# Score products ahead of the transposes of the weights, in every period of attention

## What is computed

```python
x = x + tanh(g_xattn[0]) * autocorrelation(layernorm(x), ctx, ctx)
x = x + tanh(g_ffn[0])   * routed_lora(layernorm(x))
x = x + tanh(g_xattn[1]) * attention(layernorm(x), ctx, ctx, mask)   # this one
x = x + tanh(g_ffn[1])   * fourier_ffn(layernorm(x))

# attention: 32 query heads, 8 key/value heads, width 128
q, k = rope(x @ wq), rope(ctx @ wk);  v = ctx @ wv
scores = einsum('bhgqd,bhkd->bhgqk', qg, k) / sqrt(128)
w = softmax(where(mask, scores, -1e9))
out = einsum('bhgqk,bhkd->bhgqd', w, v) @ wo
```

## Time and profile before

| | |
|---|---|
| median of 3 runs | 3050.01 us (3046.97 to 3050.73) |
| the profiled execution | 3049.93 us, of which the span is 3048.1 us |
| granted TensorE clock, mean | 0.994 of full speed |
| busy share: TensorE, VectorE, ScalarE, GpSimd | 98%, 65%, 41%, 42% |

### The profile page before, as it was taken

The page is one execution under the profiler, slowest core; times in us unless marked ns, Lnnn a source line. Parts: engine busy times, 40 slices in busy tenths (PEclk is TensorE's granted clock), DMA queues, the critical chain, the costliest instruction groups (busy, mean ns, idle before and its releaser), DMA issues.

```text
span 3048.1 us, 40952 instructions
## 1 busy us (share of the span) xinstructions
PE 2985.3 (98%) x14752; PEld 2502.7 (82%) x14752; DVE 1977.5 (65%) x4642; ACT 1256.4 (41%) x2626; POOL 1272.5 (42%) x1028
## 2 busy tenths in 40 slices
PE   9999999999999999999999999999999999999999
PEld 7888878887777878877888788888888888888887
DVE  4432478887665686678667877666766676666432
ACT  4111366665333422232224555554454445444220
POOL 2422388885322577768776333311111111111231
PEclk9999999999999999999999999999999999999999
DMA  7332421112555654455444776765566556575321
GB/s 247 127 122 97 170 57 63 70 56 100 175 193 194 194 167 111 111 157 159 111 111 125 226 239 227 242 215 169 181 206 202 181 174 218 175 272 174 136 91 56
DMA packets 317461, 479.91 MB, mean 157 GB/s; under 512 B 26108, under 2 KB 155516, under 8 KB 315468
## 3 DMA queue, kind: packets, MB, share of 16 engines
q1 hardware_dynamic: 316540, 475.84, 48.9%
q10 hardware_dynamic: 720, 1.44, 0.1%
HBM read 319.92 MB, written 157.29 MB: 157 GB/s over the span
## 4 chain that ended last, share of the span: by engine, by line
PE 56%; DVE 4%; DMA 2%; ACT 1%; POOL 1%; issue 0%; SPq 0%; ACTq 0%; DVEq 0%; POOLq 0%
PE PB L150 18%; PE PB L151 18%; PE PB L152 18%; PE PB L2383 3%; DMA at_wol<-wod 1%; DMA qp_raw<-in_wq 0%; PE PB L2682 0%; DVE qp_r L2179 0%; DMA qp_in<-xod 0%; DVE at_ptl L2522 0%; DVE at_ss L2502 0%; ACT at_ss L2430 0%; POOL qp_a L2209 0%; DVE qp_b L2142 0%; DVE qp_r L2187 0%
## 5 line engine op out<-in xcount | busy, mean ns | idle before, releaser
L2545 POOL TENSOR_TENSOR at_ql<-at_qf,at_qh 128x512 fp32r<-128x512 f32 x128 | 166.4, 1300 | 911.2 <-ACT at_qh L2423 911.2
L2430 ACT ACTIVATE at_ss<-at_ss,at_sm,at_bs 128x256 f32<-128x256 f32 x512 | 303.6, 594 | 334.8 <-DVE at_sm L2506 334.8
L150 PE MATMUL PB<-at_woh,at_ah 128*128 128x512 f32 x1024 | 400.8, 391 | 2.7 <-DMA at_wol<-wod 1.5
L151 PE MATMUL PB<-at_wol,at_ah 128*128 128x512 f32 x1024 | 399.9, 391 | 0.0
L152 PE MATMUL PB<-at_woh,at_al 128*128 128x512 f32 x1024 | 399.1, 390 | 0.0
L150 PE MATMUL PB<-qp_b,qp_a 128*128 128x512 f32 x896 | 350.0, 391 | 8.1 <-POOL qp_a L2209 2.6
L2536 DVE SCALAR_TENSOR_TENSOR at_xt<-PB,gt,at_xt 128x512 f32<-128x512 f32 x256 | 192.0, 750 | 251.7 <-PE PB L152 251.7
L152 PE MATMUL PB<-qp_b,qp_a 128*128 128x512 f32 x896 | 348.7, 389 | 0.0
L151 PE MATMUL PB<-qp_b,qp_a 128*128 128x512 f32 x896 | 348.7, 389 | 0.0
L2209 POOL TENSOR_TENSOR qp_a<-qp_raw,qp_a 128x512 fp32r<-128x512 f32 x192 | 257.8, 1354 | 104.4 <-ACT qp_a L2104 101.7
L2442 ACT ACTIVATE at_pth<-PB 128x512 fp32r<-128x512 f32 x256 | 139.4, 597 | 239.4 <-PE PB L2383 239.4
(11 more groups left out here) (290 smaller groups left out, 7466.3 us busy)
## 6 DMA issues: line engine op xcount, KB each, us to landing
at_woh<-wod SPq DMA_DIRECT2D x48, 1024.0 KB, 6.4
at_wol<-wod SPq DMA_DIRECT2D x48, 1024.0 KB, 8.9
qp_raw<-in_wq SPq DMA_DIRECT2D x32, 1024.0 KB, 5.3
qd<-qp_r SPq DMA_DIRECT2D x256, 128.0 KB, 2.5
at_qf<-qd SPq DMA_DIRECT2D x128, 256.0 KB, 3.5
at_rawo<-in_wo SPq DMA_DIRECT2D x32, 512.0 KB, 5.6
wod<-at_woh SPq DMA_DIRECT2D x16, 1024.0 KB, 5.5
wod<-at_wol SPq DMA_DIRECT2D x16, 1024.0 KB, 6.6
```

Source lines behind the costliest of these rows:

```text
L150: pe.matmul(o, ah, bh, start=start, stop=False)
L151: pe.matmul(o, ah, bl, start=False, stop=False)
L2430: m = act.activation(at_ss[s][:, c, :], at_ss[s][:, c, :], ACT.Exp, bias=z[:, 4 + c:5 + c], scale=at_bs[:, qn % 2, 8 + 2 * b + c % 2:9 + 2 ...
L2545: self.pool.tensor_tensor(at_ql[n % 3][:, :], at_qf[n % 2][:, :], asf(at_qh[n % 3][:, :]), ALU.subtract).then_inc(*inc("at_pool", ("q", n)))
```

## The change

In every period `scores(u)` is issued ahead of `turn(u - 2)`. Since all engines run the same schedule, the two steps change places on TensorE, VectorE and ScalarE alike. GpSimd and SyncE have neither step in their lists, and these stay as they are. Nothing is added or left out.

```diff
@@ -2315,10 +2315,10 @@
                 do.fetch_ahead(u)
                 if more and w == 21:
                     do.fetch_bias(qn + 1)
+                if u < NU:
+                    do.scores(u)
                 if 2 <= u < NU + 2:
                     do.turn(u - 2)
-                if u < NU:
-                    do.scores(u)
                 if more and w == 25:
                     do.bias(qn + 1)
                 if u + 2 < NU:
```

## The result

The changed kernel took 3271.37 us (median of 4, 3268.6 to 3272.7). In the same session the kernel before took 3048.49. The ratio is 1.0737, with a 95% interval of 1.0721 to 1.0753. The forecast was 3279.

The account below looks back on a forecast made before the run. TensorE, 98% busy, bounds the kernel. Plain 1241.2, rope 64.4, bias 41.4 and early 40.8 make 1387.8, less 1173.1 before is 214.7; clock 14.6 gives +229 on 3048.1, with 1.8 around it 3279 us; range 3250 to 3340.

Parts of the forecast that it names:

- The place of the cost: ScalarE: both transpose copies stand behind four exponentials, so `at_ptl` and values come late; TensorE stands 1.5 us per plain period.
- The plain period: Undisturbed attention period: 10.70 us against 9.14 before, 116 of them making 1241.2 us.
- the ten long periods: Three early, four rope and three bias periods with TensorE gaps above 3 us; eight clock falls among them, 14.6 us.
- The rope groups: Four periods with a rope group ahead of VectorE's maxima: 16.09 us each, 64.4 together; TensorE stands for 6.9.
- The bias: Three periods following 4.70 us of VectorE bias work: 13.80 us each, 41.4 together; TensorE stands over 3 us.
- The clock: TensorE's clock falls behind eight of ten long gaps, 1.82 us each, 14.6 in all; bounds 0 and 36.
- rival (a): TensorE's clock falls in plain periods too: 3350 us if one in three, 3490 if every one; chance 0.11.
- The first three periods: u = 2 to 4, without output step A to cover the values' wait: 14.0, 13.4 and 13.4 us, together 40.8.
- Rival (b): VectorE becomes the bound where GpSimd stretches its operations, in some 30 periods with `split_wo`: adds 15, 3294 us; chance 0.06.
- Rival (c): Not slower: ScalarE's copies precede output step A's end, transposes behind scores hide late softmax weights; 3045 us; chance 0.03.

Follow-up runs that it names:

- TensorE as before: Changed kernel, but TensorE keeps the old order (transposes ahead of scores), ScalarE and VectorE the new one; 3503.11 us, ratio 1.1493.
- the fill: Changed kernel plus spare 128x512 products ahead of the values in ten periods with gaps over 3 us; 3261.11 us, ratio 1.0696.
- the kernel with the late switch: Kernel before up to u = 15; from u = 16 scores first on TensorE and VectorE, ScalarE keeping copies ahead of exponentials; 3041.43 us, ratio 0.9981.
- ScalarE alone as before: Changed kernel, but ScalarE keeps the old order, copies ahead of exponentials; TensorE and VectorE in the new order; 3050.36 us, ratio 1.0009.

## Why the prediction was right, point by point

- **The place of the cost.** Right, and shown from four sides: exchanging ScalarE's steps back takes the loss away with the other engines' new order in place; halving the exponentials ahead of the copies takes 1.15 us off a period; more cover on TensorE takes the plain loss away; and delaying the scores in the period (TensorE as before) lengthens it, to 11.5 where the clock stays up.
- **The plain period.** 10.70 forecast, 10.64 measured. All links up to the values agree within 0.03. The last, from late values to the next period, was 4.16 and not the 4.23 of the earlier trace rows. The mean plain period was 10.64; over 116 periods that is 7 of the 8 us by which the forecast was high. That nothing else is left over is partly luck: the ten long periods with their falls were put at 161.2 us and took 157.3, and the three periods with the bias took 4.2 more than plain ones, which makes up for it. The points below show which way each went.
- **The rope groups.** The price of the group was too high. VectorE of the changed kernel (L2536, the first maximum) and TensorE around it:

```profile
1772.64 0.75 DVE L2536 SCALAR_TENSOR_TENSOR at_xt<-PB,gt,at_xt 128x512 f32<-128x512 f32 x1 [1.38 <-PE PB L152]
...
1777.63 0.42 DVE L2502 CUSTOM_DVE_ANT_0 at_ss<-PB,at_bi 128x256 f32<-128x256 f32 x1
```

```profile
1773.87 1.03 PE L2383 MATMUL PB<-idt,at_ss 128*128 128x128 f32 x8
...
1783.11 0.77 PE L150 MATMUL PB<-at_pth,at_vh 128*128 128x512 f32 x1 [5.47 <-DVE at_ptl L2522]
...
1790.59 1.04 PE L2383 MATMUL PB<-idt,at_ss 128*128 128x128 f32 x8
```

From L2536 to the first maximum are 4.99 us and not 6.14. L2179 ran 1.15 us in this group where it had 2118 ns on average; the prediction had a shorter group among its bounds. The values start 9.24 + 1.44 = 10.68 into the period, within 0.03 of 11.86 less the 1.15. Then the clock fell, in all four: from the values to the next transposes are 7.48 us, where a plain period has 5.60. So 16.7 to 16.9 came out. The prediction had priced the fall apart: 16.09 + 1.82 = 17.9. That a period lies near 16 is thus a short group and a fall together, and not the 16.09 as it was worked out.
- **The bias.** The period behind it was forecast at 13.80, and the pair of it and the one ahead at 24.50, without a fall. The second and the third pair took 11.30 + 13.05 = 24.35 where the long gap was filled and no fall came, so the sum was right. Its split was not: the transposes of the second period of the pair waited for the late weights too (0.5 us), which moves 0.6 into the first. In the changed kernel the second periods took 14.41 and 14.37, each with a fall. The first pair took 13.49 + 13.03 = 26.5 without one. It is 2.2 longer because one operation of the bias, L2481 (128x4), ran 2.36 us there and 0.17 in the second and the third; the last section says beside what.
- **The clock.** Eight falls in ten long gaps were forecast, 1.82 each. Read in stretches of 4 us, the clock was lowered behind nine of them: three early, four rope, two of the three behind a bias. Their prices, by the periods with and without the fill, are 1.3 to 2.8 us, the largest in u = 2 (for the rope groups 1.9 to 2.1, with the 0.67 by which the fill was too long). The plain periods kept 1.00, as the earlier trace rows had suggested, and rival (a) did not come. The run with TensorE as before shows how near it was: 2.1 us of idle time in place of 1.24, and two periods in three had the fall. The Trainium skill (TensorE: Matmul & The Clock Gate, section "A second HAM failure mode: psum-queue depth-cycling") says that frequent short idle moments make the clock swing; these runs agree at 2.1 us of idle time in each period, while at 1.24 the clock stayed at 1.00.
- **The first three periods** took 16.7, 15.0 and 16.6. With the gaps filled they were 13.92, 13.43 and 14.57, against 14.0, 13.4 and 13.4: the chain was right in two. In u = 4 of the changed kernel the shift ahead of the exponentials (L2506, 128x4), 0.16 us elsewhere, ran 1.25 (1.28 with the gaps filled) while GpSimd split a piece of `wo`. That is 1.1 of the 1.2 that the sum missed:

```profile
1680.91 2.36 POOL L2552 TENSOR_TENSOR at_wol<-at_rawo,at_woh 128x1024 fp32r<-128x1024 f32 x1 [8.38 <-ACT at_woh L2464]
...
1682.04 1.25 DVE L2506 TENSOR_TENSOR at_sm<-at_sm,at_nb 128x4 f32<-128x4 f32 x1
```

- **Rival (b)**: VectorE never became the bound; TensorE waited for nothing but `at_ptl` and, three times, the weights. **Rival (c)**: not seen, but the late weights that it spoke of are most of what the kernel with the late switch gains from.

## What to carry to other kernels

When two steps are exchanged in a schedule that all engines share, follow the exchange on each engine by itself: the step that is harmless on the busiest engine may put a long one ahead of a short one in the queue of another, and that engine's answer is what the busiest one needs next. Compare the length of that chain, from the last input it needs, with the independent work that covers it; once it is longer, the difference is paid in every period. And let the engines differ in their order where no dependence asks for the same.

## What the runs showed of the hardware

- The granted clock told two recurring gaps apart that differ by less than 1 us: idle times of 1.24 us in some 116 periods of 10.64 gave no fall, and idle times of 2.10 us in periods of 11.5 gave one in two of three, each worth 1.6 us (13.1 against 11.5). Filling 1.36 us of that gap with products whose result nobody reads made the kernel 118 us faster. The length of a gap alone does not tell: in u = 26, behind 1.36 us of idle time, the clock was 0.85 over the period with ScalarE alone as before, and 1.00 behind 1.37 us in the kernel with the late switch. Of four gaps of 2.42 or 2.43 us in the former, two had a fall and two had none.

```profile
1888.50:1899.90 11.40, 11.37 (x50) 9.23 (x51) 9.28 (x27) 5.60 (x13) 3.58 (x2) 0.85 0.62 199
```

```profile
1884.10:1894.10 10.00, 9.93 (x50) 8.02 (x51) 8.59 (x28) 5.50 (x13) 3.14 (x2) 1.00 0.56 170
```

- The first VectorE operation of a rope group (L2179, 128x512), which the change does not touch, went from 2118 ns on average to 1.15 to 1.18 us in the four groups of the changed kernel. What differs is how long GpSimd's subtraction (L2552) still runs beside it. Before and after:

```profile
1715.18 2.39 POOL L2552 TENSOR_TENSOR at_wol<-at_rawo,at_woh 128x1024 fp32r<-128x1024 f32 x1
1715.83 2.30 DVE L2179 TENSOR_TENSOR qp_r<-qp_c,qp_rope 128x512 f32<-128x512 f32 x1
```

```profile
1771.52 2.39 POOL L2552 TENSOR_TENSOR at_wol<-at_rawo,at_woh 128x1024 fp32r<-128x1024 f32 x1 [1.80 <-ACT at_woh L2464]
...
1773.31 1.15 DVE L2179 TENSOR_TENSOR qp_r<-qp_c,qp_rope 128x512 f32<-128x512 f32 x1
```

In all eight groups of these two traces L2179 ended 0.55 us behind GpSimd's operation. Where none ran beside it, as at 1719.25 with TensorE as before, it took 0.68. The trace of the changed kernel shows the same for others from 1640 us on: all 132 operations of the kinds TENSOR_TENSOR and TENSOR_SCALAR on VectorE that have no operand in PSUM (`PB`) and began during a GpSimd operation ended only behind it, among them L2506 in u = 4 and L2481 in u = 25. Operations with an operand in PSUM kept their length (`at_ptl` 0.68 us, L2536 0.75), and so did the reciprocals (L2513). The change moved VectorE's work against GpSimd's, and with it these waits. No run takes GpSimd's operation away by itself, so this rests on the traces alone.
